# Splitting the first lookup table, running TensorE beforehand and reordering the ends of a recommendation tower

## The reference

```python
e = jnp.stack([tbl_0[ids[:, 0]], ..., tbl_25[ids[:, 25]]], axis=1)
combined = jnp.concatenate([e, r_dense_x[:, None, :]], axis=1)
z = jnp.einsum('bfd,bgd->bfg', combined, combined)[:, TRIU_I, TRIU_J]
h = jnp.concatenate([z, r_dense_x], axis=1)             # 479 columns
h = jnp.maximum(h @ W_top1 + b_top1, 0.0)               # 512
h = jnp.maximum(h @ W_top2 + b_top2, 0.0)               # 256
y = h @ W_top3                                          # 1
```

## Time and profile before

| | |
|---|---|
| median of 3 runs | 365.47 us (365.24 to 366.26) |
| profiled execution | 367.2 us, of which the span from the first to the last instruction is 365.5 us |
| TensorE: matmuls / weight loads | 333.9 us (91%) / 274.7 us (75%) |
| VectorE / ScalarE / POOL | 184.6 us (50%) / 178.6 us (49%) / 261.3 us (72%) |
| mean granted TensorE clock | 0.991 |
| chain that ended last, by engine | POOL 47%, PE 31%, issue 16%, DMA 3%, ACT 2% |

### The profile page before, as it was taken

How to read it: one execution, slowest core, us unless ns; L and a number is a source line. 1 busy time by engine, 2 the same in 40 slices (tenths; PEclk the granted TensorE clock), 3 DMA queues, 4 the chain that set the end, 5 groups by cost and what they waited for, 6 DMA issues and landing times.

```text
span 365.5 us, 12436 instructions
## 1 busy us (share of the span) xinstructions
PE 333.9 (91%) x5536; PEld 274.7 (75%) x5536; DVE 184.6 (50%) x439; ACT 178.6 (49%) x234; POOL 261.3 (72%) x265
## 2 busy tenths in 40 slices
PE   1999889698999999999999999989999999988876
PEld 0488768486887888877887888867888788867675
DVE  3699954535356635465356645564365653321322
ACT  2499731544535834284435835265334835273412
POOL 6778877777777777777777777777777777777200
PEclk9999999879999999999999999999999999999999
DMA  7979493243243333334143333234243212222100
GB/s 233 344 216 250 114 299 105 54 107 95 54 124 82 81 95 95 85 79 124 52 126 86 79 94 98 78 81 115 62 121 92 66 48 73 54 52 60 37 4 3
DMA packets 19657, 37.59 MB, mean 103 GB/s; under 512 B 5557, under 2 KB 8501, under 8 KB 19604
## 3 DMA queue, kind: packets, MB, share of 16 engines
q1 hardware_dynamic: 11412, 20.00, 18.8%
q0 software_dynamic: 8192, 16.79, 17.4%
HBM read 36.77 MB, written 0.01 MB: 101 GB/s over the span
## 4 chain that ended last, share of the span: by engine, by line
POOL 47%; PE 31%; issue 16%; DMA 3%; ACT 2%; DVE 0%; DVEq 0%
POOL rows L276 47%; PE ps_lk L588 10%; PE ps_gram L614 6%; PE ps_mlp L641 3%; PE ps_zt L641 3%; DMA rows<-in_tbl,gather_ids 3%; PE ps_tr L599 3%; PE ps_zt L648 1%; PE ps_mlp L648 1%; PE ps_lk L661 1%; ACT xt L414 1%; DMA gather_ids<-in_ids_gather 1%; PE ps_lk L676 1%; PE ps_tr L676 1%; PE ps_zt L628 0%
## 5 line engine op out<-in xcount | busy, mean ns | idle before, releaser
L276 POOL DMA_INDIRECT rows<-in_tbl,gather_ids x256 | 260.0, 1016 | 78.8 <-issue 76.8
L311 DVE TENSOR_SCALAR onehot<-ids 128x512 fp32r<-128x512 f32 (+1 forms) x328 | 126.1, 440 | 74.1 <-PE ps_lk L588 41.3
L588 PE MATMUL ps_lk<-onehot,table 128*128 128x512 f32 (+1 forms) x704 | 156.3, 376 | 4.7 <-DVE onehot L311 3.6
L588 PEld LDWEIGHTS ps_lk<-onehot,table 128*128 128x128 f32 x704 | 121.3, 192 | 26.7 <-issue 4.0
L424 ACT COPY xt<-ps_tr 128x512 f32<-128x512 f32 x64 | 76.9, 1202 | 107.7 <-PE ps_tr L599 107.6
L614 PEld LDWEIGHTS ps_gram<-xt 128*26 128x26 f32 x4096 | 44.3, 103 | 23.1 <-issue 19.0
L614 PE MATMUL ps_gram<-xt 128*26 128x26 f32 x4096 | 53.7, 192 | 8.3 <-issue 3.9
L325 DVE STREAM_TRANSPOSE zs<-ps_gram 128x832 f32<-128x832 f32 x16 | 16.8, 1050 | 74.2 <-PE ps_gram L614 74.2
L411 ACT COPY xt<-ps_lk 128x512 f32<-128x512 f32 x35 | 42.0, 1235 | 20.5 <-issue 9.8
L599 PE MATMUL ps_tr<-ident,rows 128*128 128x128 f32 x256 | 39.4, 276 | 5.1 <-DMA rows<-in_tbl,gather_ids 3.3
L599 PEld LDWEIGHTS ps_tr<-ident,rows 128*128 128x128 f32 x256 | 30.1, 140 | 12.0 <-issue 5.8
(11 more groups left out here) (55 smaller groups left out, 139.3 us busy)
## 6 DMA issues: line engine op xcount, KB each, us to landing
ids<-in_ids_onehot SPq DMA_DIRECT2D x41, 256.0 KB
rows<-in_tbl,gather_ids POOLq DMA_INDIRECT x256, 3.1
w<-in_tbl SPq DMA_DIRECT2D x6, 512.0 KB, 6.8
zt<-in_tbl SPq DMA_DIRECT2D x3, 512.0 KB, 7.0
dense_x<-in_dense SPq DMA_DIRECT2D x8, 128.0 KB
zt<-in_dense SPq DMA_DIRECT2D x8, 128.0 KB, 2.4
h<-in_tbl SPq DMA_DIRECT2D x1, 512.0 KB, 6.0
w<-in_w SPq DMA_DIRECT2D x1, 512.0 KB
```

The lines of the kernel that those rows point to most:

```text
L276: pool.indirect_dma_start(rows[n % ROW_BUFS][:, r, :], None, t_[f"tbl_{GATHERED[r]}"], bass.IndirectOffsetOnAxis(ap=gather_ids[:, n, r:r + ...
L311: nc.vector.tensor_scalar(onehot[:, k, 0:w], ids[e % IDS][:, 0:w].bitcast(F32), float(k), None, ALU.is_equal).then_inc(s_unit, 1)
L588: m = nc.tensor.matmul(ps_lk[e % LB][:, x], table[:, i, part, k, :], onehot[:, k, x], start=(k == 0 and j == 0 and part == 0), stop=(k == ...
```

## The change

- Table 0 gets a high and a low part first, in two halves (`FIRST_PARTS`), and step 0 is an ordinary `lookup(0)` that waits for each half. `lookup_first` is gone. Raw tables take five staging areas in turn instead of four and one.
- TensorE runs 20 fp32 matmuls of 128 columns (`warm_up`) ahead of it, into a bank that is not yet in use.
- ScalarE makes each `high` earlier in its list, ahead of copy-outs.
- In the first tiles `gram(0,0)` stands after `turn(1,1)`, `turn(1,3)` after step 9, `gram(1,0)` between the halves of step 10, `turn_pairs(0)` ahead of `gram(1,1)`; VectorE makes the units of step 11 ahead of `pack(1)`; in chunk 1 `lookup(f)` stands ahead of `gram(a, 0)`.
- In the last chunk `last1(0, 2)` stands ahead of `gram(a + 1, 0)`.
- `finish` writes the maximum back to its PSUM bank; `kept` is gone, and TensorE waits for the finished sum (`s_y`) before it uses the bank again.

```diff
-SPLIT = list(range(1, NO)) + [0]
+FIRST_PARTS = 2
+WARM_UP = 20
...
-            def make_units(e):
-                dve.wait_ge(s_from, e + 1)
-                for k in range(KT):
+            def make_units(e, ks=range(KT)):
+                if ks[0] == 0:
+                    dve.wait_ge(s_from, e + 1)
+                for k in ks:
...
+            def low_first(part):
+                k = slice(part * KT // FIRST_PARTS, (part + 1) * KT // FIRST_PARTS)
+                dve.wait_ge(s_high, part + 1)
+                nc.vector.tensor_tensor(table[:, 0, 1, k, :], raw[0][:, k, :],
+                                        table[:, 0, 0, k, :].bitcast(F32), ALU.subtract).then_inc(s_low, 1)
...
                 if n == 0:
                     dve.wait_ge(s_base, 2)
-                else:
-                    dve.wait_ge(s_y, n)
-                dve.sem_inc(s_carrier["dve"], 1)
-                nc.vector.tensor_tensor(kept[:, :], bank[:, 0:H2], bias2[:, :], ALU.max).then_inc(s_kept, 1)
+                    dve.sem_inc(s_carrier["dve"], 1)
+                nc.vector.tensor_tensor(bank[:, 0:H2], bank[:, 0:H2], bias2[:, :], ALU.max).then_inc(s_kept, 1)
                 dve.wait_ge(s_kept, n + 1)
-                nc.vector.tensor_tensor_reduce(kept[:, :], kept[:, :], w3[:, :], 1.0, base[:, :], ALU.mult, ALU.add,
+                nc.vector.tensor_tensor_reduce(bank[:, 0:H2], bank[:, 0:H2], w3[:, :], 1.0, base[:, :], ALU.mult, ALU.add,
                                                y[:, n:n + 1]).then_inc(s_y, 1)
...
-            make_units(0)
+            make_units(0, range(0, 4))
+            low_first(0)
+            make_units(0, range(4, 6))
+            low_first(1)
+            make_units(0, range(6, KT))
...
             make_units(STEP0[1] + 2)
+            make_units(STEP0[1] + 3)
             pack(1)
-            make_units(STEP0[1] + 3)
             row_constants()
...
             shift(0)
-            high(0)
+            high_first(0)
+            high_first(1)
+            high(1)
             shift(1)
-            high(1)
+            high(2)
+            shift(2)
             evac(0)
-            shift(2)
             evac_group(0, 0)
-            high(2)
+            high(3)
             shift(3)
+            high(4)
             evac(1)
-            high(3)
...
-            def lookup_first():
-                pe.wait_ge(s_raw[0], 16)
...
+            def warm_up():
+                for _ in range(WARM_UP):
+                    nc.tensor.matmul(ps_zt[:, 0:P], ident[:, :], ident[:, :], start=True, stop=True)
+
+            def lookup(e, ks=range(KT)):
                 c, w, tables = STEPS[e]
-                if e >= LB:
+                if e >= LB and ks[0] == 0:
                     pe.wait_ge(s_lk, e - LB + 1)
...
+                if 0 < e < STEP0[1]:
+                    pe.wait_ge(s_low, split_count(tables[-1]))
+                for k in ks:
+                    if e == 0 and k % (KT // FIRST_PARTS) == 0:
+                        pe.wait_ge(s_low, k // (KT // FIRST_PARTS) + 1)
...
             pe.wait_ge(s_ident, 2)
-            lookup_first()
+            warm_up()
+            lookup(0)
...
             e = STEP0[1]
+            turn(1, 1)
             gram(0, 0)
-            turn(1, 1)
             lookup(e)
             turn(1, 2)
             gram(0, 1)
+            lookup(e + 1)
             turn(1, 3)
-            lookup(e + 1)
+            lookup(e + 2, range(0, KT // 2))
             gram(1, 0)
-            lookup(e + 2)
+            lookup(e + 2, range(KT // 2, KT))
+            turn_pairs(0)
             gram(1, 1)
...
                 if c == 1:
                     turn(a, 3)
-                gram(a, 0)
-                lookup(f)
+                    lookup(f)
+                    gram(a, 0)
+                else:
+                    gram(a, 0)
+                    lookup(f)
...
             turn(a + 1, 3)
+            last1(0, 2)
             gram(a + 1, 0)
-            last1(0, 2)
             gram(a + 1, 1)
```

More of the change, by code:

```diff
@@ L119, in build @@
         h1 = sb("h1", [P, T1, CS])
-        kept = sb("kept", [P, H2])
         bias2 = sb("bias2", [P, H2])
@@ L131, in build @@
                  for b, a, n in ((h1, 0, T1), (zt, 0, NZ + 1), (w1, 0, 2), (w1, 2, 2), (w2, 0, T1))]
-        RAWS = len(stage) - 1
-        raw = [stage[0] if j == 0 else stage[1 + SPLIT.index(j) % RAWS] for j in range(NO)]
+        RAWS = len(stage)
+        raw = [stage[j % RAWS] for j in range(NO)]
         ps_lk = [pb(f"ps_lk{i}", [P, N]) for i in range(LB)]
@@ L181, in slot, with split_count @@
             return slice(a, a + P)
+        def split_count(j):
+            return FIRST_PARTS + j
         def mlp_bank(n):
@@ L224, in load_raw @@
             def load_raw(j):
-                n = SPLIT.index(j)
-                if j > 0 and n >= RAWS:
-                    sp.wait_ge(s_low, n - RAWS + 1)
+                if j >= RAWS:
+                    sp.wait_ge(s_low, split_count(j - RAWS))
                 sp.dma_start(raw[j][:, :, :], t_[f"tbl_{ONE_HOT[j]}"].rearrange("(p k) d -> p k d", k=KT)
@@ L312, in make_units, with low @@
                                             ).then_inc(s_unit, 1)
-            def low(n):
-                j = SPLIT[n]
-                dve.wait_ge(s_high, n + 1)
+            def low_first(part):
[3 more added lines that the diff above has]
+                                        table[:, 0, 0, k, :].bitcast(F32), ALU.subtract).then_inc(s_low, 1)
+            def low(j):
+                dve.wait_ge(s_high, split_count(j))
                 nc.vector.tensor_tensor(table[:, j, 1, :, :], raw[j][:, :, :],
@@ L337, in row_constants @@
                 dve.wait_ge(s_row2, 32)
-                nc.vector.tensor_tensor_reduce(kept[:, :], bias2[:, :], w3[:, :], 1.0, 0.0, ALU.mult, ALU.add,
+                nc.vector.tensor_tensor_reduce(ps_mlp[:, 0:H2], bias2[:, :], w3[:, :], 1.0, 0.0, ALU.mult, ALU.add,
                                                base[:, :]).then_inc(s_base, 1)
@@ L358, in _ @@
             nc.vector.tensor_copy(first[:, :], first_i[:, :]).then_inc(s_first, 1)
-            make_units(0)
+            make_units(0, range(0, 4))
[3 more added lines that the diff above has]
+            make_units(0, range(6, KT))
             for e in range(1, STEP0[1]):
-                for n in range(len(STEPS[e][2])):
-                    low(STEPS[e][2][n] - 1)
+                for j in STEPS[e][2]:
+                    low(j)
                 make_units(e)
-            low(NO - 1)
             dve.wait_ge(s_const, 3)
@@ L393, in _, with high_first, high @@
         def _(act):
-            def high(n):
-                j = SPLIT[n]
+            def high_first(part):
+                k = slice(part * KT // FIRST_PARTS, (part + 1) * KT // FIRST_PARTS)
+                act.wait_ge(s_raw[0], 16)
+                nc.scalar.copy(table[:, 0, 0, k, :], raw[0][:, k, :]).then_inc(s_high, 1)
+            def high(j):
                 act.wait_ge(s_raw[j], 16)
@@ L448, in _ @@
             shift(0)
-            high(0)
+            high_first(0)
+            high_first(1)
+            high(1)
             shift(1)
-            high(1)
+            high(2)
+            shift(2)
             evac(0)
-            shift(2)
             evac_group(0, 0)
-            high(2)
+            high(3)
             shift(3)
+            high(4)
             evac(1)
-            high(3)
             shift(4)
+            high(5)
             evac(2)
             evac_group(0, 1)
-            high(4)
-            high(5)
             shift(5)
+            high(6)
             evac(3)
             evac_group(0, 2)
-            high(6)
+            high(7)
             shift(6)
+            high(8)
             evac(4)
-            high(7)
             evac_group(0, 3)
             shift(7)
+            high(9)
             evac(5)
-            high(8)
-            high(9)
             shift(8)
@@ L624, in turn_pairs @@
                 elif m > 0:
-                    pe.wait_ge(s_kept, (m - 1) * CT + 1)
+                    pe.wait_ge(s_y, (m - 1) * CT + 1)
                 flat = packed[t][:, :, :].rearrange("p k i -> p (k i)")
@@ L637, in layer1 @@
                 elif j == 0 and m > 0:
-                    pe.wait_ge(s_kept, m * CT)
+                    pe.wait_ge(s_y, m * CT)
                 for k in range(NZ + 1):
@@ L657, in last1 @@
                 elif t == 0 and j == LB:
-                    pe.wait_ge(s_kept, (CHUNKS - 1) * CT)
+                    pe.wait_ge(s_y, (CHUNKS - 1) * CT)
                 for k in range(NZ + 1 if t == 0 else NZ):
@@ L710, in _ @@
                 a, e, f = c * CT, STEP0[c], STEP0[c + 1]
-                turn_pairs(a - 2)
+                if c > 1:
+                    turn_pairs(a - 2)
                 if c == 1:
```

3 lines of the change are left out of this document (2 added, 1 removed).

## The result

The changed kernel is slower: 370.56 us as the median of 4 runs (369.67 to 371.9) beside 365.87 us for the kernel before (4 runs, 365.24 to 366.33), a ratio of 1.0132 (95% interval 1.0096 to 1.0169). The forecast was 365.9 us, at most 367.8. The profiled execution took 370.4 us with a span of 368.7.

The account below looks back on a forecast made before the run. The prediction took the gathers on POOL to bound the kernel up to 332.5 us, then a TensorE, ScalarE and VectorE chain. Terms 0 + 0 + 0 + 0.4 on 367.2 gave 367.6, carried to the median 365.9 us; range 362.0 to 367.8.

Parts of the forecast that it names:

- the warm-up: Start, on TensorE: 40 load-and-matmul pairs take 5.8 us warm or 11.6 at half clock, ending near 9 us.
- the first lookup: Start: as a high/low lookup of 16 matmuls it takes 3.93 us at full clock instead of 9.23, 5.3 less.
- the maximum in PSUM: Middle and finish: keeping it there changes two VectorE instructions; the term is 0, bounds -0.1 and +0.2 us.
- TensorE's lead: Near 10 us won at the start and first tiles is lost in longer waits for gathered rows: 0 on the path.
- The half clock that was to go: First tiles: the wait at 70.77 us and the slow lookup behind it go, about 6.0 us on TensorE.
- the instructions named: Last chunk: boundaries at instruction 7 of gram(15,0), the 5th of gram(15,1) and the 5th of last1(0,3).
- the rival in which the blocks don't bite: Last chunk: gram(15,0) and (15,1) run without a stop, last2 comes 2.9 us earlier, total 362.6 us; chance 0.24.
- +0.4 (bounds 0 and +1.4): Last chunk: late instruction blocks stop gram(15,1) and last1(0,3), so last2 ends at 354.5 us against 354.12.
- half clock late in the kernel: Sign of being wrong: lookups at half clock after a wait late in the kernel, 2.85 us each.
- The last chunk's working: last1(0,2) goes into TensorE's 1.3 us wait for the copy-out, which hides it; gram(15,0) starts 0.54 us earlier.
- The gathers, forecast at 0: Whole run: VectorE subtractions hold about as many gathers as before, so 0, between -3.8 and +5.7 us.
- the rival of a lighter hold: Gathers: subtractions hold two gathers instead of four, -1.9 us, total 364.0 us; chance 0.10.

Follow-up runs that it names:

- e1: The changed kernel with the old order of the end, last1(0,2) back between the halves of gram(15): 369.9 us, ratio 1.0093 to the kernel before.
- e2: The kernel before with only the new order of the end, last1(0,2) ahead of both halves of gram(15): 368.67 us, ratio 1.0057.
- e3: The changed kernel with 14 warm-up products instead of 20: 368.62 us, ratio 1.0035 to the kernel before.
- e6: The changed kernel with 14 warm-up products and turn(15,3) and its copy first, last1(0,1) and last1(0,2) between gram(15)'s halves: 362.61 us, ratio 0.9901 to the kernel before.
- e5: The kernel before with only the end reordered: turn(15,3) and its copy first, last1(0,1) and last1(0,2) between gram(15)'s halves: 363.49 us, ratio 0.9925.
- e7_shift_only: The kernel before with 24 small idle products (96 instructions) ahead of the first lookup, moving only the block boundaries: 374.75 us, ratio 1.0234.
- e10: The kernel before with only layer 2's maximum kept in PSUM and the wait that this takes: 365.62 us beside 366.06, ratio 0.9999.
- e8: The changed kernel with the old order of the end and no warm-up products: 365.36 us, ratio 0.9972 to the kernel before.
- e7_again: A second profile of e7_shift_only, the kernel before with 24 small products ahead of the first lookup: 377.62 us in one run.
- e11: e6 with last1(0,1) and last1(0,2) ahead of both gram halves: 363.12 us, ratio 0.9923 to the kernel before.
- e9: e6 with four dead ScalarE copies of 128x512 ahead of the copy that gram(15,0) waits for: 366.25 us.

## Why the prediction was wrong

*Where it held.* The gathers set the pace up to the last chunk and never waited for TensorE; the warm-up (6.46 us for 40 matmuls) and the first lookup (3.92) came near their prices; the maximum in PSUM is worth nothing. TensorE's lead was lost ahead of the end, as forecast, but not as described: its waits for rows grew only from 3.3 us to 6.9, the longest of them at 45.56 and not around 90 to 116 us. The half clock that was to go, worth about 6.0 us, stayed: 6.8 us long ahead of the end in both profiles, from 70 us on in that of before, at 46 and 87 us in that of the changed kernel. The boundaries lay at the instructions named, and the rival in which the blocks don't bite is refuted by the profile.

*The step that failed* is the last chunk, "+0.4 (bounds 0 and +1.4)". It measured +4.71, from the last turn to the finish. Its stops were sized fairly: work resumed some 3.3 and 3.5 us after the blocks were entered, against 2.92 and 3.25, and stops and cover together come to +1.05 of the 4.71. The other 3.66 is a term that the sum did not have: half clock behind the 2.05 us stop. The prediction had that price in hand, for it read 6.78 us against 3.93 for the same lookup at half clock after an idle stretch, and named half clock late in the kernel among the things that would prove it wrong. It then priced two new stops as bare idle time. e1, e2 and e3 show the term in three more orders and positions, e6 what the end costs without it. What sets it off in one execution and not in another stays open, as said above.

*Cover that was given away.* The last chunk's working let the copy wait hide last1(0,2), and it does. But between the gram halves that product had hidden 1.16 us of the next block's way: without it the stop went from 1.27 us (before) to 2.02 (e2), and with the new front from 1.17 (e1) to 2.05 (the changed kernel). The sum had this in its times and did not say it: the product moved from one wait into another.

*Two smaller terms.* gram(14,1) was to fall from 1.80 to 1.26 and start gram(15,0) 0.54 earlier; it took 1.71, and gram(15,0) came 1.90 us after the last turn, as before. The gathers, forecast at 0, came 1.7 us earlier at the end, just past the 1.5 us that the prediction allowed. Fewer held gathers are not the reason: four of about 1.9 us or more stand in both profiles. Much of the 1.7 belongs to the one profile of before: in e2, e5, e7_shift_only and e10, which have the old front, the last gather starts at 337.8 to 338.9 us, and in the profiles with the new front at 337.2 to 338.4. e8 puts the front's worth at 1.1 us, a little over half the price of the rival of a lighter hold; by what way it comes is not shown.

*The page.* The two stops of the changed kernel, 2.05 and 1.33 us, and that of 3.89 in e7_again are further against what the Trainium skill, "Runtime: NRT & Kernel Launch", section "Instruction fetch mechanics", says of crossings, that their cost is mostly hidden; here the measurement decides. Its refill in blocks of 256 agrees with every stop placed beforehand in e1 to e8.

## What to carry to other kernels

When a change adds, removes or moves instructions on an engine that runs hundreds of very short ones, count where the block boundaries fall in its densest stretches, and keep longer products just ahead of and between them (and, if the reading of e3 and e11 above holds, no semaphore wait); here that was worth 3 us without changing any work (e5). Price a stop of TensorE as its length plus what half clock may add to everything behind it until the clock is back (3.66 us here, nothing behind the stop put into e9), and look for that in the granted clock before looking for a cause in the order of the work. Filler is not free because its engine idles at that moment: 20 warm-up products or none in the first 8 us moved the end by some 4.5 us (e1 and e8).

## What was not expected of the hardware

When a block arrives varies between kernels with one and the same TensorE program, and an early stop can reach the end. The windows of 86 to 88 us and the product behind them, in e6 and in e9:

```profile
86.00:88.00 2.00, 1.89 (x115) 1.41 (x115) 1.68 (x5) 0.00 (x0) 1.39 (x3) 1.00 0.47 145
```

```profile
89.32 0.29 PE L621 MATMUL ps_gram<-xt 128*26 128x26 f32 x12 [1.08 <-issue]
```

```profile
86.00:88.00 2.00, 1.91 (x109) 1.42 (x109) 1.76 (x5) 0.00 (x0) 1.39 (x3) 1.00 0.69 160
```

```profile
90.06 0.29 PE L623 MATMUL ps_gram<-xt 128*26 128x26 f32 x12 [1.76 <-issue]
```

The longer stop stands beside busier DMA engines (share 0.69 against 0.47), as does that of 3.89 us in e7_again (0.97 from 88 to 90 us); no run varied that load by itself. The block's own packet moves 2.3 to 2.4 us ahead of the restart in all three profiles (at 87.0 us in e6, 87.6 in e9, 90.6 in e7_again), so the difference arises before the packet moves and not on its way. TensorE never made up the 2.4 us in e9, since from there the gathers' pace and its own agree: from tile 4 to tile 12 e6 takes 165.7 us for the gathers and 165.3 for the turns. That the gathers set the time holds only as long as TensorE still meets waits for rows, and in e6 the last of these is at 239 us.
